# Building a scan's operands on ScalarE instead of GpSimd, in a fused Mamba2, MLP and LoRA kernel

## The chip, the cores and the metric

The kernel runs on one core of one Trainium2 chip. The metric is the device time in microseconds (us) of one execution. Three executions of the kernel before took 840.97, 840.18 and 839.14 us, median 840.18. One more execution was profiled: 837.98 us, of which 836.1 us are the span from the first to the last recorded instruction; all rows of the trace come from it.

## The reference

The input is 8 sequences of 256 tokens with 512 features. A Mamba2 block, a gated MLP and a linear layer with one of four LoRA experts per token follow each other, with residuals and normalizations. The change touches the Mamba2 block alone, in which (H = 4 heads, P = N = 128, chunks of Q = 128 tokens, and `Xc` the same for all heads):

```
z, xs, Bs, Cs, dt = split(x @ w_in.T);  xBC = silu(conv(xBC) + conv_b)
dt = softplus(dt + dt_bias);  a = dt * A;  cs = cumsum(a)
Ldec = where(tri, exp(cs[q] - cs[k]), 0);  Xdt = Xc * dt
Yd = (C @ B.T * Ldec) @ Xdt;   states = sum_q exp(cs[-1] - cs) * B * Xdt
Yo = C @ prev * exp(cs);       Y = Yd + Yo + D * xh
y = Y * silu(z) @ w_out.T
```

## The kernel before

There is one group per sequence (`GROUPS` = 8), that is two tiles of 128 tokens. Each matrix product is made of three f16 products of high and low halves. The work is a software pipeline of three stages over groups: stage a is the Mamba2 block, b the gated MLP, c the linear layer with LoRA. `first()` runs stage a of group 0 alone, together with the preparation of the weights; it is called the head below. Then `steps` runs t = 1 to 9, with a of group t, b of group t-1 and c of group t-2. Stage a exists in the head and in steps 1 to 7. Step 1 also prepares most of the MLP's weights: `prepare(f)` has ScalarE write the upper f16 halves (L560) and VectorE the lower ones (L871).

A step has FBLK = 14 blocks, f = 0 to 13. In each block TensorE makes the gate and up products of block f (`b_gu`, 24 matmuls into the PSUM banks `gu`) and then the down product of block f-1 (`b_down`, 6 matmuls into `acc`). Between them lie ScalarE's silu (L670, tile `sg`), VectorE's product (L1044), ScalarE's upper half of the activation (L680, tile `act`) and VectorE's lower half (L1049). `b_down(f)` waits for that lower half of block f (`act_ready`). The pieces of stages a and c are hung behind these in each block by the tables `A_AT` and `C_AT`, one table for each engine. All engines run their own list strictly in the order in which it is written, and semaphores tie the lists together; nothing is scheduled by a planner.

The pieces of stage a that matter here are these.

- `a_dt` on ScalarE and VectorE (f = 2) turns the projected dt into dt (`dts`) and a = dt*A (`a_t`, L978), 8 numbers in each partition: 2 tiles of 4 heads.
- `a_scan_in` on GpSimd (L453) multiplies the triangular mask `tri` by `a_t`, to `ra`, one 128x512 operation for each tile: the operand of the matmul that makes the sums of a (`a_dec` on TensorE, f = 4 and 5, which waits for `ra_ready`, and outside the head for `sz_ready`, ScalarE's silu of z, for the bank).
- `a_tdt` on GpSimd (L461) multiplies `tri` by dt, to `tdt`, which lies in the tile `hn`; VectorE multiplies it with the exponentials (`a_dec`, f = 5).
- `a_xd` on GpSimd (L469) makes D * xh, four 128x256 operations into `y`, added much later (`a_y`, f = 7, L1005).
- ScalarE has at f = 3 `a_silu(g, 2)`, `a_z(g, 1)` and `a_tok` (L608, L614, L627), and at f = 4 the two exponentials (`a_exp`, L638), for which it loads another table of functions and then the first again (ACT_TABLE_LOAD).
- `a_xw` and `a_ce` on GpSimd (L476, L484) make the operands of the state. TensorE's `a_state` (f = 6, `wa<-hn,tok`) waits for `xw_ready`.

Of the kernel before, what the change touches and what calls it, by code (L numbers as in the profile page):

```python
# [24 lines left out]
ALU = mybir.AluOpType  # L25
ACT = mybir.ActivationFunctionType
# [8 lines left out]
H = 4  # L35
# [67 lines left out]
def build(nc, x, w_in, w_dt, w_out, w_gate, w_up, w_down, w_lin, w_gl, lora_b, cols, rows, ln_rows, out):  # L103
# [3 lines left out]
    with ctx:  # L107
# [8 lines left out]
        def sem(name):  # L116
            if name not in made:
                made[name] = ctx.enter_context(nc.semaphore(name))
            return made[name]
# [199 lines left out]
        def prev(g, per, k, eng, s):  # L319

            if g > 0:
                eng.wait_ge(s, g * per - per + k)
# [94 lines left out]
        def _(pool):  # L417
# [27 lines left out]
                inv_std(chain_n, s_a[:, 1], mv_a[:, :, 1], 1.0 + EPS, EPS * EPS, sem("rstd2_a_ready"))  # L445
                inv_std(chain_n, s_a[:, 0], mv_a[:, :, 1], 1.0, EPS, sem("rstd_a_ready"))

            def a_scan_in(g):
                pool.wait_ge(sem("a_ready"), g + 1)
                for j in range(TILES):  # L450
                    if j == 0:
                        prev(g, 3, 3, pool, sem("dec_ps_ready"))
                    nc.gpsimd.tensor_tensor(ra[:, j], tri[:].unsqueeze(1).broadcast_to([P, H, P]),  # L453
                                            a_t[:, j].unsqueeze(2).broadcast_to([P, H, P]), ALU.mult)\
                        .then_inc(sem("ra_ready"), 1)

            def a_tdt(g):


                for j in range(TILES):  # L460
                    nc.gpsimd.tensor_tensor(tdt[:, j], tri[:].unsqueeze(1).broadcast_to([P, H, P]),  # L461
                                            dts[:, 4, j].unsqueeze(2).broadcast_to([P, H, P]), ALU.mult)\
                        .then_inc(sem("tdt_ready"), 1)

            def a_xd(g):
                prev(g, 2, 2, pool, sem("o_ps_ready"))
                pool.wait_ge(sem("xbc_ready"), g * 3 + 1)
                for h in range(H):
                    nc.gpsimd.tensor_scalar(y[:, h], xbc[:, 0], rowt[:, 4 + h:5 + h], None, ALU.mult)\  # L469
                        .then_inc(sem("xd_ready"), 1)  # L470

            def a_xw(g):
                pool.wait_ge(sem("w0_ready"), g + 1)
                pool.wait_ge(sem("tok_ready"), g + 1)
# [30 lines left out]
            def step(a, b, c):  # L505
                if c is not None:
                    chain_c.group(c)
                    norm_c(c, 1, 1.0)
                if b is not None:
                    b_copy(b)  # L510
                if a is not None:
                    a_xd(a)
                    a_scan_in(a)
                    a_tdt(a)
                if c is not None:
                    norm_c(c, 2, ACT_SCALE)
                if a is not None:
                    a_xw(a)
                    a_ce(a)
                    if a + 1 < GROUPS:  # L520
                        a_norm(a + 1)
                    a_rms(a)
                if c is not None:
                    norm_c(c, 3, 1.0)
                    chain_c.close()

            def first():
                a_norm(0)
                a_scan_in(0)
                a_tdt(0)  # L530
                a_xd(0)
                a_xw(0)
                a_ce(0)
                a_norm(1)
                a_rms(0)
# [6 lines left out]
        def _(eng):  # L542
# [74 lines left out]
            def a_dt(g):  # L617
# [3 lines left out]
                chain_a(nc.scalar.activation(dts[:, 2], dts[:, 1], ACT.Exp, scale=-1.0))  # L621
                nc.scalar.activation(dts[:, 3], dts[:, 2], ACT.Ln, bias=1.0).then_inc(sem("log_ready"), 1)

            def a_tok(g):
                eng.wait_ge(sem("tok_ps_ready"), g + 1)
                prev(g, 2, 2, eng, sem("y_ps_ready"))
                nc.scalar.activation(tok[:].rearrange("p m s -> p (m s)"), bank(g, 2)[:, 0:3 * P], ACT.Copy)\  # L627
                    .then_inc(sem("tok_ready"), 1)
# [72 lines left out]
            def c_u(g, j):  # L701
# [2 lines left out]

            A_AT = {0: lambda g: a_conv(g, 1), 1: lambda g: (a_conv(g, 2), a_silu(g, 0)),
                    2: lambda g: (a_silu(g, 1), a_z(g, 0), a_dt(g)),
                    3: lambda g: (a_silu(g, 2), a_z(g, 1), a_tok(g)),
                    4: lambda g: (a_exp(g, 0), a_exp(g, 1)), 6: lambda g: (a_exp(g, 2), a_state(g)),
                    8: lambda g: a_sumsq(g, 0), 9: lambda g: a_sumsq(g, 1), 11: lambda g: a_hi2(g)}
            NEXT_AT = {10: lambda g: a_hi1(g), 13: lambda g: a_conv(g, 0)}  # L710
# [21 lines left out]
            def first():  # L732
                chain_a.group(0)
                prep_a()
                a_t1(0)
                small_hi(T_IN)
                upper_halves(range(0, 9))
                a_conv(0, 0)
                upper_halves([9])
                a_dt(0)  # L740
                a_silu(0, 0)
                a_conv(0, 1)
                a_conv(0, 2)
                a_tok(0)
                a_exp(0, 0)
                a_exp(0, 1)
                a_exp(0, 2)
                a_silu(0, 1)
                a_silu(0, 2)
                a_z(0, 0)  # L750
                a_z(0, 1)
                upper_halves(range(S_GU, S_GU + 4))
                a_state(0)
                upper_halves(range(S_GU + 4, S_GU + 7))
                a_sumsq(0, 0)
                a_sumsq(0, 1)
                upper_halves(range(S_GU + 7, S_MIX))
                a_hi1(1)
                a_t2(0)
                a_conv(1, 0)  # L760
                chain_a.close()
# [857 lines left out]
```

## Time and profile before

| What | us |
|---|---|
| median of three executions | 840.18 |
| profiled execution | 837.98 |
| its span | 836.1 |
| TensorE busy | 770.9 |
| VectorE busy | 478.1 |
| ScalarE busy | 331.5 |
| GpSimd busy | 150.0 |

In the trace TensorE is PE (its weight loads PEld), VectorE DVE, ScalarE ACT and GpSimd POOL; L with a number is a line of the kernel. Step 1 runs from about 76 to 172 us. The token transposes of steps 2 to 7 start at 201.05, 296.19, 391.32, 486.46, 579.93 and 675.07 us, 95.1 us apart, and once 93.5 us. A share of busy time says little here, because each engine's list is in fixed order: what counts is, in each block, which wait ends last.

### The profile page before, as it was taken

Reading aid. Unit: us, or ns where it says so; the run is one execution under the profiler, and the core shown is the slowest. Engines: PE = TensorE matmul, PEld = TensorE weight load, DVE = VectorE, ACT = ScalarE, POOL = GpSimd, SP = SyncE. Lnnn points to the kernel's source line nnn. Section 1 sums busy time; section 2 is a strip of 40 time slices with the busy share of each in tenths; the row PEclk is TensorE's granted clock in tenths of the full one; section 3 lists DMA queues with packets and bytes.
Section 4 is the critical chain, followed back from the end, with each engine's and each line's share of the span. In section 5 each row is a group of like instructions: output and inputs, shape, how many; then the busy total and the mean of one; then the engine's idle time right before and its main releaser. Section 6 shows DMA issues by size and latency. Waiting matters only on the chain.

```text
span 836.1 us, 13857 instructions
## 1 busy us (share of the span) xinstructions
PE 770.9 (92%) x5558; PEld 540.1 (65%) x5558; DVE 478.1 (57%) x1109; ACT 331.5 (40%) x603; POOL 150.0 (18%) x197
## 2 busy tenths in 40 slices
PE   4994989999999999999999999999999999999945
PEld 3853856676657866586666866677666866577632
DVE  6874667875635665475645565465644564265163
ACT  2642676625423443324523453325523353222211
POOL 1420121214110331014110331014110320010010
PEclk9995999999999999999999999999999999999987
DMA  9931000300104020210104020210103110021010
GB/s 331 387 131 26 1 26 1 67 11 26 26 2 97 5 51 1 52 52 26 26 1 78 25 51 1 51 51 21 33 1 63 39 27 1 11 66 27 1 50 26
DMA packets 59936, 41.11 MB, mean 49 GB/s; under 512 B 45664, under 2 KB 45792, under 8 KB 59872
## 3 DMA queue, kind: packets, MB, share of 16 engines
q1 hardware_dynamic: 59872, 40.22, 17.4%
q8 instruction: 44, 0.72, 0.4%
q14 instruction: 20, 0.16, 0.1%
HBM read 25.01 MB, written 4.19 MB: 35 GB/s over the span
## 4 chain that ended last, share of the span: by engine, by line
PE 80%; DVE 10%; ACT 4%; issue 2%; DMA 2%; SPq 1%; POOL 0%; POOLq 0%; DVEq 0%; ACTq 0%
PE gu L1252 32%; PE wa L1252 22%; PE acc L1252 17%; PE wc L1252 7%; DVE xbc L944 2%; DVE weights L871 2%; ACT L621 1%; DMA weights<-in_w_in 1%; ACT silu_z L614 1%; DVE sg L1044 0%; DVE stats_c L886 0%; DVE dts L970 0%; PE wa L1340 0%; DVE h L1074 0%; DMA xa<-in_x 0%
## 5 line engine op out<-in xcount | busy, mean ns | idle before, releaser
L1252 PE MATMUL gu<-h2t,weights 128*128 128x256 f16 x2688 | 320.2, 277 | 0.0
L1252 PEld LDWEIGHTS gu<-h2t,weights 128*128 128x128 f16 x2688 | 264.5, 99 | 58.4 <-issue 19.7
L1252 PE MATMUL acc<-weights,act 128*128 128x512 f16 x672 | 163.4, 379 | 5.8 <-DVE act L1049 5.8
L1044 DVE SCALAR_TENSOR_TENSOR sg<-gu,bound,sg 128x256 f32<-128x256 f32 x112 | 53.7, 480 | 136.9 <-ACT sg L670 136.8
L670 ACT ACTIVATE sg<-gu,scale_inv 128x256 f32<-128x256 f32 x112 | 52.9, 472 | 172.9 <-PE gu L1252 172.8
L1252 PE MATMUL wa<-ht,weights 128*128 128x256 f16 x912 | 110.3, 280 | 5.3 <-DMA ht<-ra 5.3
L1252 PEld LDWEIGHTS wa<-ht,weights 128*128 128x128 f16 x912 | 91.4, 100 | 23.9 <-DMA ht<-ra 5.7
L1252 PEld LDWEIGHTS acc<-weights,act 128*128 128x128 f16 x672 | 65.3, 98 | 63.2 <-DVE act L1049 7.9
L680 ACT ACTIVATE act<-sg 128x256 f16<-128x256 f32 x112 | 46.6, 416 | 98.4 <-DVE sg L1044 97.6
L1049 DVE TENSOR_TENSOR act<-sg,act 128x256 f16<-128x256 f32 x112 | 52.0, 464 | 54.0 <-ACT act L680 54.0
L944 DVE SCALAR_TENSOR_TENSOR xbc<-wa,conv_ws,xbc 128x253 f32<-128x253 f32 (+1 forms) x132 | 57.3, 475 | 3.0 <-ACT xbc L597 1.5
L439 POOL TENSOR_SCALAR small_c<-mv_c 128x2 f32<-128x2 f32 x24 | 4.6, 191 | 303.3 <-DVE mv_c L888 303.3
L1252 PE MATMUL wa<-w_out_t,y 128*128 128x512 f32 x128 | 57.4, 592 | 0.0
L871 DVE SCALAR_TENSOR_TENSOR weights<-weights,scale_v 128x512 f16<-128x512 f32 x56 | 41.1, 790 | 15.6 <-ACT weights L560 15.5
L469 POOL TENSOR_SCALAR y<-xbc,rows_t 128x256 f32<-128x256 f32 x32 | 36.1, 1140 | 43.9 <-ACT xbc L608 43.9
L597 ACT ACTIVATE xbc<-wa,cols_t,conv_ws 128x256 f32<-128x256 f32 x48 | 24.4, 559 | 47.2 <-PE wa L1252 47.2
L1252 PEld LDWEIGHTS wa<-w_out_t,y 128*128 128x128 f32 x128 | 24.2, 190 | 25.5 <-issue 23.4
L1252 PE MATMUL wc<-weights,h3t 128*128 128x512 f16 x168 | 38.5, 379 | 0.0
L560 ACT ACTIVATE weights<-weights,scale_v 128x512 f16<-128x512 f32 x56 | 36.2, 711 | 0.9 <-DVE scale_v L821 0.5
L648 ACT ACTIVATE hn<-h 128x512 f32<-128x512 f32 x16 | 10.1, 631 | 61.5 <-DVE h L1012 61.5
L1012 DVE TENSOR_TENSOR h<-wa,h 128x512 f32<-128x512 f32 x16 | 11.0, 690 | 35.3 <-PE wa L1252 35.3
L453 POOL TENSOR_TENSOR ra<-tri,a_t 128x512 f32<-128x512 f32 x16 | 17.2, 1094 | 68.9 <-DVE a_t L978 68.9
(194 smaller groups left out, 790.4 us busy)
## 6 DMA issues: line engine op xcount, KB each, us to landing
xa<-in_x SPq DMA_DIRECT2D x8, 512.0 KB, 3.5
weights<-in_x SPq DMA_DIRECT2D x8, 512.0 KB, 3.7
out_x<-h SPq DMA_DIRECT2D x16, 256.0 KB, 2.2
weights<-in_w_in SPq DMA_DIRECT2D x5, 512.0 KB, 6.5
weights<-in_w_down SPq DMA_DIRECT2D x3, 768.0 KB, 13.2
weights<-in_w_gate SPq DMA_DIRECT2D x2, 1024.0 KB, 12.7
weights<-in_w_up SPq DMA_DIRECT2D x2, 1024.0 KB, 14.1
weights<-in_w_gate SPq DMA_DIRECT2D x2, 768.0 KB, 14.3
```

What stands on the lines that cost most here:

```text
L453: nc.gpsimd.tensor_tensor(ra[:, j], tri[:].unsqueeze(1).broadcast_to([P, H, P]), a_t[:, j].unsqueeze(2).broadcast_to([P, H, P]), ALU.mult)\
L469: nc.gpsimd.tensor_scalar(y[:, h], xbc[:, 0], rowt[:, 4 + h:5 + h], None, ALU.mult)\
L560: nc.scalar.activation(Wh[:, u, 0], W[:, u + SHIFT], ACT.Copy, scale=sv[:, t:t + 1])\
L597: nc.scalar.activation(xbc[:, c], src[:, m * SEQ:(m + 1) * SEQ], ACT.Identity, bias=conv_b[:, c:c + 1], scale=cw[:, c * TAPS + TAPS - 1:c ...
L670: nc.scalar.activation(sg[:, f % 2], GU[f % 2][:, 0:SEQ], ACT.Silu, scale=inv_gate)\
L680: nc.scalar.activation(act[:, slot(f), 0], sg[:, f % 2], ACT.Copy)\
L871: nc.vector.scalar_tensor_tensor(Wh[:, u, 1], W[:, u + SHIFT], sv[:, t:t + 1], Wh[:, u, 0], ALU.mult, ALU.subtract).then_inc(split, 1)
L944: ins = nc.vector.scalar_tensor_tensor(xbc[:, c, late:], conv_in(g, c)[:, 0:SEQ - late], cw[:, c * TAPS + k:c * TAPS + k + 1], xbc[:, c, l ...
L1012: nc.vector.tensor_tensor(h01[:, j], o_bank(g, j)[:], h01[:, j], ALU.add)\
L1044: nc.vector.scalar_tensor_tensor(sg[:, f % 2], GU[f % 2][:, SEQ:2 * SEQ], up_to_act, sg[:, f % 2], ALU.mult, ALU.mult).then_inc(sem("prod_ ...
L1049: nc.vector.tensor_tensor(act[:, slot(f), 1], sg[:, f % 2], act[:, slot(f), 0], ALU.subtract)\
L1252: return nc.tensor.matmul(dst, left, right, start=start, stop=stop)
```

## The change

`a_scan_in`, `a_tdt` and `a_xd` leave GpSimd's list and enter ScalarE's. ScalarE takes a scale for each partition, so each head and tile becomes an operation of its own: 8 copies of 128x128 for `ra`, 8 for `tdt`, and 4 of 128x256 for D * xh. GpSimd keeps `a_xw`, `a_ce`, the copies of `h1b` and the small powers. In the steps all 20 copies stand at f = 3: 16 ahead of `a_silu(g, 2)` and 4 behind `a_tok`. In the head the 16 stand between `a_tok` and the first exponential, the 4 behind `a_z`. The wait of `a_scan_in` for `dec_ps_ready` of the group before is gone. The lists of TensorE, VectorE and SyncE are unchanged.

```diff
--- before.py
+++ after.py
@@ -445,30 +445,6 @@
                 inv_std(chain_n, s_a[:, 1], mv_a[:, :, 1], 1.0 + EPS, EPS * EPS, sem("rstd2_a_ready"))
                 inv_std(chain_n, s_a[:, 0], mv_a[:, :, 1], 1.0, EPS, sem("rstd_a_ready"))
 
-            def a_scan_in(g):
-                pool.wait_ge(sem("a_ready"), g + 1)
-                for j in range(TILES):
-                    if j == 0:
-                        prev(g, 3, 3, pool, sem("dec_ps_ready"))
-                    nc.gpsimd.tensor_tensor(ra[:, j], tri[:].unsqueeze(1).broadcast_to([P, H, P]),
-                                            a_t[:, j].unsqueeze(2).broadcast_to([P, H, P]), ALU.mult)\
-                        .then_inc(sem("ra_ready"), 1)
-
-            def a_tdt(g):
-
-
-                for j in range(TILES):
-                    nc.gpsimd.tensor_tensor(tdt[:, j], tri[:].unsqueeze(1).broadcast_to([P, H, P]),
-                                            dts[:, 4, j].unsqueeze(2).broadcast_to([P, H, P]), ALU.mult)\
-                        .then_inc(sem("tdt_ready"), 1)
-
-            def a_xd(g):
-                prev(g, 2, 2, pool, sem("o_ps_ready"))
-                pool.wait_ge(sem("xbc_ready"), g * 3 + 1)
-                for h in range(H):
-                    nc.gpsimd.tensor_scalar(y[:, h], xbc[:, 0], rowt[:, 4 + h:5 + h], None, ALU.mult)\
-                        .then_inc(sem("xd_ready"), 1)
-
             def a_xw(g):
                 pool.wait_ge(sem("w0_ready"), g + 1)
                 pool.wait_ge(sem("tok_ready"), g + 1)
@@ -508,10 +484,6 @@
                     norm_c(c, 1, 1.0)
                 if b is not None:
                     b_copy(b)
-                if a is not None:
-                    a_xd(a)
-                    a_scan_in(a)
-                    a_tdt(a)
                 if c is not None:
                     norm_c(c, 2, ACT_SCALE)
                 if a is not None:
@@ -526,9 +498,6 @@
 
             def first():
                 a_norm(0)
-                a_scan_in(0)
-                a_tdt(0)
-                a_xd(0)
                 a_xw(0)
                 a_ce(0)
                 a_norm(1)
@@ -621,6 +590,27 @@
                 chain_a(nc.scalar.activation(dts[:, 2], dts[:, 1], ACT.Exp, scale=-1.0))
                 nc.scalar.activation(dts[:, 3], dts[:, 2], ACT.Ln, bias=1.0).then_inc(sem("log_ready"), 1)
 
+            def a_scan_in(g):
+                eng.wait_ge(sem("a_ready"), g + 1)
+                for j in range(TILES):
+                    for h in range(H):
+                        ins = nc.scalar.activation(ra[:, j, h], tri[:], ACT.Copy, scale=a_t[:, j, h:h + 1])
+                    ins.then_inc(sem("ra_ready"), 1)
+
+            def a_tdt(g):
+
+                for j in range(TILES):
+                    for h in range(H):
+                        ins = nc.scalar.activation(tdt[:, j, h], tri[:], ACT.Copy, scale=dts[:, 4, j, h:h + 1])
+                    ins.then_inc(sem("tdt_ready"), 1)
+
+            def a_xd(g):
+                prev(g, 2, 2, eng, sem("o_ps_ready"))
+                eng.wait_ge(sem("xbc_ready"), g * 3 + 1)
+                for h in range(H):
+                    nc.scalar.activation(y[:, h], xbc[:, 0], ACT.Copy, scale=rowt[:, 4 + h:5 + h])\
+                        .then_inc(sem("xd_ready"), 1)
+
             def a_tok(g):
                 eng.wait_ge(sem("tok_ps_ready"), g + 1)
                 prev(g, 2, 2, eng, sem("y_ps_ready"))
@@ -704,7 +694,7 @@
 
             A_AT = {0: lambda g: a_conv(g, 1), 1: lambda g: (a_conv(g, 2), a_silu(g, 0)),
                     2: lambda g: (a_silu(g, 1), a_z(g, 0), a_dt(g)),
-                    3: lambda g: (a_silu(g, 2), a_z(g, 1), a_tok(g)),
+                    3: lambda g: (a_scan_in(g), a_tdt(g), a_silu(g, 2), a_z(g, 1), a_tok(g), a_xd(g)),
                     4: lambda g: (a_exp(g, 0), a_exp(g, 1)), 6: lambda g: (a_exp(g, 2), a_state(g)),
                     8: lambda g: a_sumsq(g, 0), 9: lambda g: a_sumsq(g, 1), 11: lambda g: a_hi2(g)}
             NEXT_AT = {10: lambda g: a_hi1(g), 13: lambda g: a_conv(g, 0)}
@@ -742,6 +732,8 @@
                 a_conv(0, 1)
                 a_conv(0, 2)
                 a_tok(0)
+                a_scan_in(0)
+                a_tdt(0)
                 a_exp(0, 0)
                 a_exp(0, 1)
                 a_exp(0, 2)
@@ -749,6 +741,7 @@
                 a_silu(0, 2)
                 a_z(0, 0)
                 a_z(0, 1)
+                a_xd(0)
                 upper_halves(range(S_GU, S_GU + 4))
                 a_state(0)
                 upper_halves(range(S_GU + 4, S_GU + 7))
```

The changed kernel's rows carry its own line numbers (its L660 is L670 before, for example). First ScalarE at blocks f = 3 and 4 of step 2 (`sg` is the MLP's silu, `act` its activation's upper half, `xbc` the convolution's silu, `dec` the exponentials). Before:

```order
L670 ACTIVATE sg<-gu,scale_inv 128x256
L680 ACTIVATE act<-sg 128x256
L608 ACTIVATE xbc<-xbc 128x512
L614 ACTIVATE silu_z<-wa,scale_inv 128x512
L627 ACTIVATE tok<-wa 128x384
L670 ACTIVATE sg<-gu,scale_inv 128x256
L680 ACTIVATE act<-sg 128x256
L638 ACT_TABLE_LOAD
L638 ACTIVATE dec<-wa 128x512 x2
```

And in the changed kernel:

```order
L660 ACTIVATE sg<-gu,scale_inv 128x256
L670 ACTIVATE act<-sg 128x256
L597 ACTIVATE ra<-tri,a_t 128x128 x8
L604 ACTIVATE hn<-tri,dts 128x128 x8
L577 ACTIVATE xbc<-xbc 128x512
L583 ACTIVATE silu_z<-wa,scale_inv 128x512
L617 ACTIVATE tok<-wa 128x384
L611 ACTIVATE y<-xbc,rows_t 128x256 x4
L660 ACTIVATE sg<-gu,scale_inv 128x256
L670 ACTIVATE act<-sg 128x256
L628 ACT_TABLE_LOAD
L628 ACTIVATE dec<-wa 128x512 x2
```

Twenty operations more stand between the `act` of block 3 and the `sg` of block 4. In steps 3 to 7 the piece reads the same, and in step 1 three `weights` operations stand behind `tok` before and behind `y` now.

Then ScalarE in the head, from the copy of the transposed tokens (`tok`) to that of the state (`act<-wa`, L643 before). Before:

```order
L627 ACTIVATE tok<-wa 128x384
L638 ACT_TABLE_LOAD
L638 ACTIVATE dec<-wa 128x512 x2
L638 ACTIVATE act<-wa 128x512
L608 ACT_TABLE_LOAD
L608 ACTIVATE xbc<-xbc 128x512 x2
L614 ACTIVATE silu_z<-gu,scale_inv 128x512 x2
L560 ACTIVATE weights<-weights,scale_v 128x512 x4
L643 ACTIVATE act<-wa 128x512
```

And in the changed kernel:

```order
L617 ACTIVATE tok<-wa 128x384
L597 ACTIVATE ra<-tri,a_t 128x128 x8
L604 ACTIVATE hn<-tri,dts 128x128 x8
L628 ACT_TABLE_LOAD
L628 ACTIVATE dec<-wa 128x512 x2
L628 ACTIVATE act<-wa 128x512
L577 ACT_TABLE_LOAD
L577 ACTIVATE xbc<-xbc 128x512 x2
L583 ACTIVATE silu_z<-gu,scale_inv 128x512 x2
L611 ACTIVATE y<-xbc,rows_t 128x256 x4
L529 ACTIVATE weights<-weights,scale_v 128x512 x4
L633 ACTIVATE act<-wa 128x512
```

The table load for the exponentials, which stood right behind `tok`, now stands behind the sixteen copies, and the four copies for `y` stand ahead of the weights' halves.

## Rows read from the trace of the kernel before

**Rows 1.** The page: busiest engine, and the chain that ended last, by engine.
```profile
PE 770.9 (92%) x5558; PEld 540.1 (65%) x5558; DVE 478.1 (57%) x1109; ACT 331.5 (40%) x603; POOL 150.0 (18%) x197
...
PE 80%; DVE 10%; ACT 4%; issue 2%; DMA 2%; SPq 1%; POOL 0%; POOLq 0%; DVEq 0%; ACTq 0%
```
**Rows 2.** Waits of PE: for whom, us in total, times, longest.
```profile
PE wa L1340 <- DVE xbc L944: 14.5, 7, 2.1
```
**Rows 3.** PE timeline, step 3: start, us, instructions, [idle before <-releaser].
```profile
296.54 4.45 PE L1252 MATMUL gu<-h2t,weights 128*128 128x256 f16 x24
...
306.46 1.46 PE L1252 MATMUL acc<-weights,act 128*128 128x512 f16 x6
...
312.09 1.46 PE L1252 MATMUL acc<-weights,act 128*128 128x512 f16 x6
...
314.25 1.02 PE L1252 MATMUL wa<-hn,tok 128*128 128x512 f32 x2
```
**Rows 4.** ACT timeline, step 3: the silu of blocks 4 and 5.
```profile
301.03 0.47 ACT L670 ACTIVATE sg<-gu,scale_inv 128x256 f32<-128x256 f32 x1 [2.68 <-PE gu L1252]
...
307.21 0.47 ACT L670 ACTIVATE sg<-gu,scale_inv 128x256 f32<-128x256 f32 x1
```
**Rows 5.** DVE and POOL timelines, step 3, block 5.
```profile
308.69 0.43 DVE L1049 TENSOR_TENSOR act<-sg,act 128x256 f16<-128x256 f32 x1 [0.48 <-ACT act L680]
...
310.00 1.54 POOL L476 TENSOR_TENSOR hn<-tok,w 128x512 f32<-128x512 f32 x1 [8.68 <-DVE w L992]
```
**Rows 6.** ACT groups by form: xcount, busy us, mean ns of one, idle before.
```profile
L680 ACT ACTIVATE act<-sg 128x256 f16<-128x256 f32 x112 | 46.6, 416 | 98.4 <-DVE sg L1044 97.6 <-PE acc L1252 0.8
...
L581 ACT ACTIVATE ra<-dec,small_a 128x512 f16<-128x512 f32 x14 | 9.2, 710 | 0.0
...
L686 ACT ACTIVATE weights<-h 128x512 f16<-128x512 f32 x14 | 8.0, 629 | 0.9 <-DVE h L1074 0.9
...
L552 ACT ACTIVATE gl_w<-h3t 128x144 f16<-128x144 f32 x1 | 0.3, 322 | 1.3 <-DVE h3t L848 1.3
```
**Rows 7.** ACT timeline, head: two scaled copies in a row.
```profile
67.67 1.32 ACT L581 ACTIVATE ra<-dec,small_a 128x512 f16<-128x512 f32 x2
```
**Rows 8.** Windows of steps 3 and 5 (third from last: PEclk), ACT and PE timelines of step 5.
```profile
296.00:302.00 6.00, 5.81 (x33) 4.16 (x34) 4.18 (x10) 2.36 (x5) 2.47 (x4) 0.72 0.29 90
...
486.00:492.00 6.00, 5.54 (x36) 3.96 (x37) 5.00 (x12) 3.43 (x7) 2.75 (x4) 1.00 0.23 81
...
489.64 0.47 ACT L670 ACTIVATE sg<-gu,scale_inv 128x256 f32<-128x256 f32 x1 [1.01 <-PE gu L1252]
...
502.86 1.02 PE L1252 MATMUL wa<-hn,tok 128*128 128x512 f32 x2
```
**Rows 9.** Timelines of step 1: DVE, POOL, ACT and PE, blocks 3 to 6.
```profile
109.24 3.27 DVE L871 SCALAR_TENSOR_TENSOR weights<-weights,scale_v 128x512 f16<-128x512 f32 x3
...
115.46 2.08 DVE L871 SCALAR_TENSOR_TENSOR weights<-weights,scale_v 128x512 f16<-128x512 f32 x3 [0.75 <-ACT weights L560]
...
108.81 2.49 POOL L461 TENSOR_TENSOR hn<-tri,dts 128x512 f32<-128x512 f32 x2
...
126.70 1.55 POOL L476 TENSOR_TENSOR hn<-tok,w 128x512 f32<-128x512 f32 x1 [15.41 <-DVE w L992]
...
116.55 0.46 ACT L670 ACTIVATE sg<-gu,scale_inv 128x256 f32<-128x256 f32 x1
...
125.88 1.47 PE L1252 MATMUL acc<-weights,act 128*128 128x512 f16 x6 [0.58 <-DVE act L1049]
...
128.39 1.10 PE L1252 MATMUL wa<-hn,tok 128*128 128x512 f32 x2 [0.19 <-POOL hn L476]
```
**Rows 10.** ACT and PE timelines, head: table load, first exponential, attention products.
```profile
36.25 1.28 ACT L638 ACT_TABLE_LOAD   x1
39.86 0.60 ACT L638 ACTIVATE dec<-wa 128x512 f32<-128x512 f32 x1 [2.33 <-PE wa L1252]
...
44.88 1.96 PE L1252 MATMUL wa<-xbc 128*128 128x512 f32 x4 [0.19 <-ACT xbc L608]
```

## The prediction

> **What bounds the kernel now.** I read the page first. TensorE is busy for 92% of the span, and 80% of the chain that ended last is TensorE's own work [rows 1]. So its list is almost never empty, and time is lost where it waits. The view of waits gives the one wait of the steady steps: seven times about 2.1 us at the token transposes, for VectorE's convolution [rows 2], which follows the dt chain of block 2. GpSimd has no part in it. So the work that the change takes from GpSimd is not what TensorE waits for, and the question is what the same work does to ScalarE.
>
> For this I read the timelines of one steady step (step 3, blocks 3 to 6). ScalarE sits idle 2.68 us before the silu of block 4 [rows 4]. Its silu of block 5 starts at 307.21, the lower half of that block's activation is done at 308.69 + 0.43 = 309.12 on VectorE [rows 5], and TensorE asks for it at 312.09 [rows 3]: a margin of 2.9 us, not counting 0.07 us of signal. Behind this, GpSimd's first product for the state runs from 310.00 to 311.54 [rows 5] and TensorE's state matmul stands at 314.25 [rows 3]. These margins are what the change spends.
>
> **The price of the new operations.** The trace has no 128x128 copy on ScalarE with a scale for each partition. The rows around it give one [rows 6]: a plain copy takes 629 ns at 512 columns and 416 at 256, so 0.83 ns for a column and 203 ns fixed; at 128 columns that is 309 ns (the 128x144 copy, 322 ns, lies on this line). The same 512 columns with a scale from a tile take 710, that is 81 ns more. So one copy lasts about 390 ns at 128 columns and 497 at 256. Two scaled copies in a row take 1.32 us and not 1.42 [rows 7]: back to back each costs 0.10 us less. I take 0.29 us for a 128x128 copy and 0.40 for a 128x256 one. From below: the scale might cost nothing on these shapes, then 0.21 and 0.32. From above: the plain 128x144 copy plus 0.10 for the scale, less only 0.09 of overlap, 0.33, and 0.42 for the larger. My values lie on the line through four rows, so I stay with them. The insertion at block 3 is X = 16 x 0.29 + 4 x 0.40 = 6.24 us (4.6 to 7.0 by the bounds).
>
> **The head.** Here the table load for the exponentials ran at 36.25, while ScalarE would have waited anyway, and 2.33 us of idling were left before the first exponential [rows 10]. Now 16 x 0.29 = 4.64 us come first and the load behind them. The exponential moves by 4.64 - 2.33 = 2.31 us. The third exponential, the second table load and the silu follow in a row, and TensorE's attention products waited for that silu even before, by 0.19 us at 44.88 [rows 10]. TensorE's list is in order, so everything behind moves: **+2.31**. The four copies for D stand in front of weights' halves and a state copy that waits for TensorE anyway: nothing. VectorE's convolution, relieved of GpSimd beside it, ends earlier, but then waits for TensorE's gram products: nothing.
>
> **Step 1.** ScalarE has no idle time here: the weights' halves fill it, and the silu of block 4 starts at 116.55 with no gap [rows 9]. TensorE already waits 0.58 us for the activation of block 5 at 125.88, and 0.19 us for GpSimd's product at 128.39 [rows 9]. So all of X reaches TensorE. One thing comes back. GpSimd's multiplication of the mask by dt ran at 108.81 beside three of VectorE's lower halves, which took 3.27 us where the same three take 2.08 at 115.46 [rows 9]. They stood ahead of the product of block 3, and ScalarE waited for it before its next work. That is -1.19 us. Step 1: 6.24 - 1.19 = **+5.05**.
>
> **Steps 2 to 7.** In step 3 TensorE runs the gate and up product of block 4 in 4.45 us [rows 3]. The granted clock in that window is 0.72 of full speed, in step 5 it is 1.00 [rows 8], after the same wait of 2.1 us: the clock fell to 1.2 GHz in the one and stayed at 2.4 GHz in the other. Windows at steps 2, 4, 6 and 7 read much like step 3. So there are five steps of one kind and one of the other.
>
> With the drop: the silu of block 4 had 2.68 us of idling before it, 2.78 with the overlap that copies in a row regain. It moves by 6.24 - 2.78 = 3.46 us. The activation of block 4 has about 3.5 us to TensorE's 306.46 [rows 3] and is just in time. Everything to block 5's silu is one row of ScalarE work with two table loads, so that silu goes to 307.21 + 3.46 = 310.67. The down product of block 5 finds its operand at 309.12 + 0.07 + 3.46 = 312.65 and not at 312.09: +0.6. The state matmul needs GpSimd's product, which ended at 311.54 and took 0.14 us to be seen (126.70 + 1.55 to 128.39 in step 1 [rows 9]). It now comes at 311.68 + 3.46 = 315.14, against 314.25: **+0.89** in all for the step. Nothing gives it back: up to the next transposes TensorE was never idle, and the dt chain that these wait for starts from TensorE's own products.
>
> Without the drop (step 5): the idle time before the silu of block 4 was only 1.01 us [rows 8], 1.11 with the overlap. The silu moves by 5.13, from 489.64 to 494.77; block 5's silu follows 6.18 us later as in step 3 (307.21 - 301.03 [rows 4]), at 500.95; the state's operand follows 311.68 - 307.21 = 4.47 us behind that, at 505.42, against 502.86 [rows 8]: **+2.56**. A step with the drop was 1.7 us longer than one without, and the added costs differ by as much: both kinds become equally long, because ScalarE's row of work sets the end in each.
>
> **Sum.** 2.31 + 5.05 + 5 x 0.89 + 2.56 = 14.4 us. On the profiled execution that is 837.98 + 14.4 = 852.4, on the median of the runs, 2.2 us higher, 854.6. With the low prices (X = 4.6): head 16 x 0.21 - 2.33 = 1.0, step 1 3.4, steps with the drop 0 (they cost from X = 5.35 on), step 5 0.9, together 5.4. With the high prices (X = 7.0): 2.95 + 5.8 + 5 x 1.65 + 3.3 = 20.3. These ends are 845.6 and 860.5.
>
> **Rivals.**
> *The new copies are cheaper* and the margins of steps 2 to 7 hold. For it: no row shows a small scaled copy, and the margin is missed by less than 1 us. Against it: four rows lie on one line. Price: +5.4, so 845.6; it holds while X is under 5.35.
>
> *The clock pays too.* In step 1 TensorE would wait for the second sum (its bank is freed by the silu of z, now behind the 16 copies), for block 4 and for block 5, some 3.2, 2.5 and 2.3 us within 17. After one wait of 2.1 us it fell to half rate in five of seven cases, and 24 matmuls then took 4.45 us for 2.78 (the row at 296.54 [rows 3]). A drop under ScalarE's row costs nothing, since TensorE then waits less; one behind it costs 1.67 us. At four to seven more of these: +7 to +12, so 862 to 867. Against it: the new waits of the steady steps are below 1 us. The Trainium skill, TensorE: Matmul & The Clock Gate, section HAM oscillation, says that idle gaps inside a loop make the engine fall back to half rate every time round. By this rule it could be paid in each step; no row shows it after a wait as short as the new ones.
>
> *Faster: VectorE gains what GpSimd gives up, and ScalarE's insertion hides.* One place on the path pays, the three halves of step 1: -1.19, so 839.0. It decides only if X in step 1 is below 1.19 us, that is 0.06 us a copy, and the head's sixteen fit into 2.33 us. Against it stands every row of ScalarE. The Trainium skill speaks for this rival: GPSIMD Engine Reference, section Specifications, says that GpSimd shares its SBUF interfaces with VectorE and contends with instructions that have two SBUF inputs or run in a two-port mode. The 3.27 against 2.08 us agree with it. But in steps 2 to 7 it meets only work with slack, or with an operand in PSUM.
>
> *Nothing to see*: waits that I take for binding are not, and slack elsewhere swallows all: within 1.7 us of 840.18. Only GpSimd's own path could hide that much, and it is not in the chain [rows 1].
>
> **Chances.** Forecast (850 to 860.5, its own mechanism at prices near mine) 0.70; cheaper copies (843 to 850) 0.14; clock (above 860.5) 0.11; no difference 0.03; faster 0.02. A change of 0.2%, 1.7 us, is about what a measurement of this kernel can tell. So faster 0.02, same 0.03, slower 0.95. The range takes in the bounds of the copies' prices, 846 to 861.
>
> **What would show it.** ScalarE's groups should have 128 copies of 128x128 at about 390 ns and 32 of 128x256 at about 500. PE should get a new wait for ACT at the first attention products in the head, of 2.5 us; in step 1 waits for VectorE's `act` before the down products of blocks 4 and 5; in each later step about 0.6 us before the down product of block 5 and 0.3 before the state matmul. Steps 2 to 7 should all be 96.0 us long, with a clock drop or without. The three lower halves at block 3 of step 1 should take 2.08 us. The forecast is wrong if the steady steps keep 95.1 us (the copies are cheap), or if they reach 98 (clock, or a link of the row that I hold to be free).

## The result and the profile after

The changed kernel takes 854.64 us in the median of four executions (854.21 to 855.14). The kernel before took 839.66 in the four executions beside it. The ratio is 1.0186, 95% interval 1.0152 to 1.0219: slower by 1.5 to 2.2%. The profiled execution took 854.21 us, span 852.5, against 837.98 and 836.1 before.

The chain's shares by engine, and TensorE's waits, on the page and in the view of waits:

```profile
PE 773.1 (91%) x5558; PEld 537.1 (63%) x5558; DVE 471.5 (55%) x1109; ACT 381.1 (45%) x763; POOL 79.8 (9%) x133
...
PE 66%; ACT 14%; DVE 12%; issue 4%; DMA 2%; POOL 2%; SPq 1%; POOLq 0%; DVEq 0%; ACTq 0%
```
```profile
PE wa L1333 <- DVE xbc L937: 14.6, 7, 2.1
...
PE acc L1245 <- DVE act L1042: 8.0, 12, 1.6
PE wa L1245 <- ACT silu_z L583: 7.8, 5, 3.0
...
PE wa L1245 <- ACT dec L628: 2.2, 1, 2.2
...
PE wa L1245 <- POOL hn L452: 1.3, 7, 0.2
```

GpSimd lost 70 us of work and ScalarE won 50. TensorE's share of the chain fell from 80% [rows 1] to 66%, and ScalarE's rose from 4 to 14%. The wait of [rows 2] is unchanged. What is new are waits for ScalarE, directly (`silu_z`, `dec`) or through VectorE and GpSimd, which only pass its delay on. The five waits for `silu_z` are one of 2.97 us in step 1 and one of 1.2 us in each of the four later steps whose clock did not drop.

ScalarE's new groups by form (xcount | busy us, mean ns):

```profile
L597 ACT ACTIVATE ra<-tri,a_t 128x128 f32<-128x128 f32 x64 | 19.4, 386 | 0.0
L604 ACT ACTIVATE hn<-tri,dts 128x128 f32<-128x128 f32 x64 | 19.4, 386 | 0.0
...
L611 ACT ACTIVATE y<-xbc,rows_t 128x256 f32<-128x256 f32 x32 | 13.6, 498 | 0.0
```

Back to back, eight of the small ones take 2.43 us, 0.292 each beyond the first, and four of the large ones 1.70, 0.40 each. So X, the prediction's name for the length of all 20 copies in the row of block 3, was 6.27 us.

Step 3 on TensorE, and the silu of blocks 4 and 5 on ScalarE, as in [rows 3] and [rows 4]:

```profile
306.06 4.45 PE L1245 MATMUL gu<-h2t,weights 128*128 128x256 f16 x24
...
322.17 1.47 PE L1245 MATMUL acc<-weights,act 128*128 128x512 f16 x6 [0.39 <-DVE act L1042]
...
324.69 0.67 PE L1245 MATMUL wa<-hn,tok 128*128 128x512 f32 x1 [0.19 <-POOL hn L452]
```
```profile
314.04 0.46 ACT L660 ACTIVATE sg<-gu,scale_inv 128x256 f32<-128x256 f32 x1
...
320.21 0.47 ACT L660 ACTIVATE sg<-gu,scale_inv 128x256 f32<-128x256 f32 x1
```

ScalarE's silu of block 4 has no idle time in front of it any more. The two new waits of TensorE are those that the margins of [rows 5] let expect. The printed idle is shorter than the real delay, because a row's printed length reaches past the start of the next row (24 matmuls are printed as 2.78 us and the next row starts 2.62 behind them). From start to start the two delays are 0.55 and 0.36 us, and with the state matmuls, which are 0.08 us longer, 0.99 in all.

The table takes the time from the token transposes of one step to those of the next as the length of a step. A clock drop, here and below, is a stretch in which the clock granted to TensorE fell to its lower level (1.2 GHz) behind the transposes.

| Stretch | before | after | difference | predicted |
|---|---|---|---|---|
| start to the head's transposes | 35.21 | 35.62 | +0.4 | 0 |
| from there to step 1's (rest of the head, start of step 1) | 74.26 | 77.29 | +3.0 | +2.3 |
| step 1 to 2 | 91.58 | 96.67 | +5.1 | +5.05 |
| step 2 to 7, five | 474.02 | 480.67 | +6.65 | +6.1 |
| step 7 to the end | 161.03 | 162.25 | +1.2 | +0.9 |

The sum is 16.4 us in these two profiled executions, and 15.0 between the medians. All five steps after are 96.12 to 96.14 us long, although behind the transposes the clock fell in steps 3 and 4 and in none of the other five (windows at steps 3 and 5, granted clock third from last; compare [rows 8]):

```profile
306.00:312.00 6.00, 6.00 (x34) 4.14 (x32) 2.78 (x7) 6.00 (x19) 0.88 (x2) 0.72 0.26 90
...
498.00:505.00 7.00, 5.78 (x36) 3.84 (x37) 3.00 (x8) 6.75 (x21) 0.88 (x2) 1.00 0.29 76
```

Step 1 on VectorE and TensorE, to be read with [rows 9]:

```profile
112.68 2.07 DVE L864 SCALAR_TENSOR_TENSOR weights<-weights,scale_v 128x512 f16<-128x512 f32 x3
```
```profile
116.11 1.47 PE L1245 MATMUL acc<-weights,act 128*128 128x512 f16 x6
...
121.41 1.15 PE L1245 MATMUL wa<-ra,below 128*128 128x512 f32 x2 [2.97 <-ACT silu_z L583]
122.37 4.45 PE L1245 MATMUL gu<-h2t,weights 128*128 128x256 f16 x24
127.40 1.47 PE L1245 MATMUL acc<-weights,act 128*128 128x512 f16 x6 [0.58 <-DVE act L1042]
...
134.38 1.47 PE L1245 MATMUL acc<-weights,act 128*128 128x512 f16 x6 [1.17 <-DVE act L1042]
```

The lower halves are back at 2.07 us with GpSimd silent. With that a wait of TensorE ahead of the down product of block 3 is gone, which the kernel before had:

```profile
113.86 1.47 PE L1252 MATMUL acc<-weights,act 128*128 128x512 f16 x6 [1.25 <-DVE act L1049]
```

The wait for the bank (2.97 us) was followed by a fall of the clock (granted clock 0.72 from 121 to 127 us). The 24 matmuls behind it took 4.45 us and not 2.78, and that filled most of what would have been the next wait.

The head, on ScalarE and TensorE, to be read with [rows 10]:

```profile
38.88 2.43 ACT L604 ACTIVATE hn<-tri,dts 128x128 f32<-128x128 f32 x8
41.33 1.28 ACT L628 ACT_TABLE_LOAD   x1
42.62 1.09 ACT L628 ACTIVATE dec<-wa 128x512 f32<-128x512 f32 x2
```
```profile
43.27 1.52 PE L1245 MATMUL wa<-ra,ones 128*128 128x512 f32 x2 [2.18 <-ACT dec L628]
...
45.44 3.69 PE L1245 MATMUL gu<-ht,weights 128*128 128x256 f16 x24
```

The table load, once inside ScalarE's idle time, now stands behind the copies, and TensorE waits 2.18 us for the first exponential. Behind that wait the clock fell too (granted clock 0.82 from 40 to 46 us): the 24 matmuls took 3.69 us for 2.78, and the rows in front of them were slower as well. From the head's transposes to the attention products it is 13.34 us (35.62 to 48.96), and was 9.67 before (35.21 to 44.88): 3.7 us more, of which some 1.3 are the clock. The trace of the run with D*xh back on GpSimd, described below, has the same wait without the fall:

```profile
44.36 1.12 PE L1247 MATMUL wa<-ra,ones 128*128 128x512 f32 x2 [2.18 <-ACT dec L631]
...
45.76 2.78 PE L1247 MATMUL gu<-ht,weights 128*128 128x256 f16 x24
48.73 1.96 PE L1247 MATMUL wa<-xbc 128*128 128x512 f32 x4 [0.19 <-ACT xbc L587]
```

There it is 12.02 us (36.71 to 48.73), 2.35 more than before.

### The profile page after: what moved, and what is told of

It is laid out like the page before. It is cut to its first block, busy times and chain, and to the rows that moved or that the text cites. A ratio compares the mean times of both kernels' runs of the same rounds, so it can differ in the third digit from the quotient of the medians.

```text
span 852.5 us, 13946 instructions
## 1 busy us (share of the span) xinstructions
PE 773.1 (91%) x5558; PEld 537.1 (63%) x5558; DVE 471.5 (55%) x1109; ACT 381.1 (45%) x763; POOL 79.8 (9%) x133
## 4 chain that ended last, share of the span: by engine, by line
PE 66%; ACT 14%; DVE 12%; issue 4%; DMA 2%; POOL 2%; SPq 1%; POOLq 0%; DVEq 0%; ACTq 0%
PE gu L1245 26%; PE wa L1245 19%; PE acc L1245 14%; PE wc L1245 7%; DVE xbc L937 2%; ACT hn L604 2%; ACT ra L597 2%; DVE sg L1037 1%; DVE weights L864 1%; ACT y L611 1%; POOL hn L452 1%; ACT L628 1%; ACT L660 1%; ACT L590 1%; ACT silu_z L583 1%
## 5 line engine op out<-in xcount | busy, mean ns | idle before, releaser
L1245 PE MATMUL gu<-h2t,weights 128*128 128x256 f16 x2688 | 316.8, 275 | 0.0
L660 ACT ACTIVATE sg<-gu,scale_inv 128x256 f32<-128x256 f32 x112 | 52.9, 472 | 132.2 <-PE gu L1245 131.2
L670 ACT ACTIVATE act<-sg 128x256 f16<-128x256 f32 x112 | 46.6, 416 | 112.3 <-DVE sg L1037 112.3
L1042 DVE TENSOR_TENSOR act<-sg,act 128x256 f16<-128x256 f32 x112 | 47.7, 426 | 54.1 <-ACT act L670 54.1
L864 DVE SCALAR_TENSOR_TENSOR weights<-weights,scale_v 128x512 f16<-128x512 f32 x56 | 38.7, 747 | 21.9 <-ACT weights L529 21.8
L1245 PEld LDWEIGHTS wc<-weights,h3t 128*128 128x128 f16 x168 | 16.4, 98 | 19.8
```

The lines of the kernel that those rows point to most:

```text
L660: nc.scalar.activation(sg[:, f % 2], GU[f % 2][:, 0:SEQ], ACT.Silu, scale=inv_gate)\
L670: nc.scalar.activation(act[:, slot(f), 0], sg[:, f % 2], ACT.Copy)\
L864: nc.vector.scalar_tensor_tensor(Wh[:, u, 1], W[:, u + SHIFT], sv[:, t:t + 1], Wh[:, u, 0], ALU.mult, ALU.subtract).then_inc(split, 1)
L1042: nc.vector.tensor_tensor(act[:, slot(f), 1], sg[:, f % 2], act[:, slot(f), 0], ALU.subtract)\
L1245: return nc.tensor.matmul(dst, left, right, start=start, stop=stop)
```

## Experiments

Two theories were tested. "Row" is the prediction's: ScalarE's work of block 3 is one uninterrupted row, and its length X, against fixed margins, sets the cost. "Share" is that each copy on ScalarE costs its part wherever it stands. Times are medians; ratio is against runs of the kernel before on the same chip (838.3 to 839.2 us, 839.66 for the changed kernel). What is said of single steps comes from one profiled execution of each kernel.

| Kernel | us | ratio (95%) | step with / without clock drop |
|---|---|---|---|
| before | 839.66 | 1 | 95.1 / 93.5 |
| changed | 854.64 | 1.0186 (1.0152 to 1.0219) | 96.1 / 96.1 |
| D*xh back on GpSimd | 845.98 | 1.0089 (1.0065 to 1.0112) | 95.1 / 94.95 |
| only D*xh on ScalarE | 838.66 | 0.9993 (0.9983 to 1.0003) | 95.1 / 93.5 |
| D*xh at block 5 | 846.94 | 1.0092 (1.0072 to 1.0112) | 95.1 / 94.96 |
| and the 16 copies last | 843.70 | 1.0076 (1.0048 to 1.0103) | 95.1 / 94.5 |
| eight copies more | 873.18 | 1.0409 (1.0393 to 1.0426) | 99.0 in all |
| head as before | 852.21 | 1.0161 (1.0136 to 1.0186) | 96.1 / 96.1 |
| tdt held in step 1 | 837.00 | 0.9981 (0.9966 to 0.9997) | 95.1 / 93.5 |
| before, turned | 815.29 | 0.9719 (0.9696 to 0.9743) | no drop, 91.2 |
| changed, turned | 835.22 | 0.9964 (0.9947 to 0.9980) | no drop, 93.5 |
| before, turned and held | 815.69 | 0.9734 (0.9710 to 0.9759) | no drop, 91.2 |

**D*xh back on GpSimd.** `a_xd` as before, `a_scan_in` and `a_tdt` on ScalarE.

> The changed kernel, with D*xh given back to GpSimd (32 copies of 128x256 less on ScalarE; the 128 copies of 128x128 stay). Theory 'row': ScalarE's insertion at block 3 has the length X, 6.27 us in the changed kernel and 16 x 0.292 = 4.67 us here. A step with a clock drop pays only what is above 5.35, so nothing: steps of 95.1 us; one without a drop pays X - 3.68 = 1.0. The head still pays its 3.0 us, step 1 pays 4.67 - 1.19 = 3.5. Sum 6.5 to 9 us over the kernel before, about 847. Theory 'share' (each copy on ScalarE costs its share wherever it stands, 14 to 16 us over 160 copies, 0.1 us each): 128 copies, 12 us over before, about 852.

7.5 us over before (5.5 to 9.4), as "row" says and not the 12 of "share". One fifth of the copies, a quarter of X, carried half of the cost, because it was the part above the margin. The one step without a drop took 94.95 us, where 94.5 were expected (see D*xh at block 5).

**Only D*xh on ScalarE.**

```diff
-                    a_xd(a)
...
-                a_xd(0)
...
-                    3: lambda g: (a_silu(g, 2), a_z(g, 1), a_tok(g)),
+                    3: lambda g: (a_silu(g, 2), a_z(g, 1), a_tok(g), a_xd(g)),
...
+                a_xd(0)
```

> The kernel before, with D*xh alone moved to ScalarE (32 copies of 128x256, behind a_tok at block 3, behind a_z in the head). Theory 'row': X = 1.6 us. Step 1, where ScalarE has no idle time, pays 1.6; the head and steps 2 to 7 pay nothing (95.1 us, or 93.5 where the clock does not fall). About +1.6 us over before. Theory 'share': 32 copies at 0.1 us, +3.2 us, spread over head and steps: steps of 95.5 us.

The trace has what was expected: step 1 is 203.83 - 110.66 = 93.17 us and was 91.58, the others are unchanged.

```profile
110.66 0.52 PE L1339 MATMUL wa<-ident,xbc 128*128 128x128 f32 x3 [2.08 <-DVE xbc L943]
...
203.83 0.52 PE L1339 MATMUL wa<-ident,xbc 128*128 128x128 f32 x3 [2.08 <-DVE xbc L943]
```

The time has not: 0.6 us less than before (1.4 less to 0.3 more), where 1.6 more was expected. In the profiled execution two of steps 2 to 7 had no clock drop and not one, which is 1.7 us. Whether the later steps go without it more often in this kernel is not settled, since only profiled executions show single steps.

**D*xh at block 5.** The same 160 copies.

```diff
-                    3: lambda g: (a_scan_in(g), a_tdt(g), a_silu(g, 2), a_z(g, 1), a_tok(g), a_xd(g)),
-                    4: lambda g: (a_exp(g, 0), a_exp(g, 1)), 6: lambda g: (a_exp(g, 2), a_state(g)),
+                    3: lambda g: (a_scan_in(g), a_tdt(g), a_silu(g, 2), a_z(g, 1), a_tok(g)),
+                    4: lambda g: (a_exp(g, 0), a_exp(g, 1)), 5: lambda g: a_xd(g),
+                    6: lambda g: (a_exp(g, 2), a_state(g)),
```

> The changed kernel with the same 160 copies, but in the steps the four for D*xh stand at block 5, behind the activation of block 5, where ScalarE was idle for 3.6 us. Theory 'row': the row up to the state's operand loses 1.6 us, so X = 4.67 in front of it: steps with a drop 95.1 us, without 94.5, step 1 pays 3.5 and the head 3.0 as in the kernel with D*xh on GpSimd: about 847, 6.5 to 9 us over before. Theory 'share': no change against the changed kernel, 854.6, steps of 96.1.

7.7 us less than the changed kernel with as many copies: "share" is out. One number was off. Steps without a drop took 94.96 us, not 94.5, and the timeline of TensorE in step 6 names another link, the wait for the silu of z that frees the bank:

```profile
588.75 0.52 PE L1334 MATMUL wa<-ident,xbc 128*128 128x128 f32 x3 [2.09 <-DVE xbc L938]
...
595.25 1.13 PE L1246 MATMUL wa<-ra,below 128*128 128x512 f32 x2 [1.22 <-ACT silu_z L583]
...
683.71 0.52 PE L1334 MATMUL wa<-ident,xbc 128*128 128x128 f32 x3 [2.09 <-DVE xbc L938]
```

**The 16 copies last**, behind `a_silu`, `a_z` and `a_tok`, with D*xh at block 5. Against the changed kernel:

```diff
-                    3: lambda g: (a_scan_in(g), a_tdt(g), a_silu(g, 2), a_z(g, 1), a_tok(g), a_xd(g)),
-                    4: lambda g: (a_exp(g, 0), a_exp(g, 1)), 6: lambda g: (a_exp(g, 2), a_state(g)),
+                    3: lambda g: (a_silu(g, 2), a_z(g, 1), a_tok(g), a_scan_in(g), a_tdt(g)),
+                    4: lambda g: (a_exp(g, 0), a_exp(g, 1)), 5: lambda g: a_xd(g),
+                    6: lambda g: (a_exp(g, 2), a_state(g)),
```

> The changed kernel with D*xh at block 5, and at block 3 the 16 copies behind a_silu(g, 2), a_z(g, 1) and a_tok instead of ahead of them. The amount of work up to the silu of block 4 is the same as with D*xh at block 5 alone (X = 4.67), only the silu of z, which frees the bank of TensorE's second sum, comes 4.7 us earlier. Two links are to be told apart for a step without a clock drop, which took 94.96 us there. If the bank is the link (wait of 1.22 us), it becomes 93.5 + (4.67 - 3.68) = 94.5 us and the wait is gone; steps with a drop stay at 95.1. If the row to the state's operand is the only link, nothing changes. In all about 846, 0 to 2 us less than with D*xh at block 5 alone.

Step 6 is now 681.97 - 587.44 = 94.53 us, and the bank's wait is gone; the block-5 wait is what is left:

```profile
587.44 0.52 PE L1334 MATMUL wa<-ident,xbc 128*128 128x128 f32 x3 [2.08 <-DVE xbc L938]
...
602.29 1.47 PE L1246 MATMUL acc<-weights,act 128*128 128x512 f16 x6 [0.38 <-DVE act L1043]
...
681.97 0.52 PE L1334 MATMUL wa<-ident,xbc 128*128 128x128 f32 x3 [2.08 <-DVE xbc L938]
```

So there are two links: the silu of z behind the 16 copies, which sets a step without a drop at X = 4.67, and the row to the state's operand, which sets the changed kernel's steps. In all the kernel is 3.2 us quicker than with D*xh at block 5 alone, where 0 to 2 were expected. Three steps without a drop explain 0.4 us each, 1.3 together. In the profiled executions 0.8 us more lie ahead of step 1's transposes, where the clock fell in the head of that run (24 matmuls in 4.43 us) and not of this one (2.78), and 1.2 behind step 7's, for a cause that is open.

**Eight copies more**, into a spare tile that nobody reads.

```diff
...
+                    for j in range(TILES):
+                        for h in range(H):
+                            nc.scalar.activation(spare[:, j, h], tri[:], ACT.Copy, scale=a_t[:, j, h:h + 1])\
...
```

> The changed kernel with eight more 128x128 copies a step (into a spare f16 tile, read by nobody) behind the eight for ra, steps 1 to 7 only. Theory 'row': above the knee each us of X is a us of step: 8 x 0.292 = 2.34 us for each of seven steps, 16.4 over the changed kernel, 871; steps 2 to 7 of 98.5 us each, with a clock drop or without. Theory 'share': 56 copies at 0.1 us, +5.6, 860.

18.5 us over the changed kernel, 16.4 expected. A step takes 98.97 us, 2.84 more for 2.34 us of copies. The rest is the first link and the clock, as steps 2 and 4 show:

```profile
222.58 1.71 PE L1253 MATMUL wa<-ra,below 128*128 128x512 f32 x2 [3.55 <-ACT silu_z L584]
224.09 3.92 PE L1253 MATMUL gu<-h2t,weights 128*128 128x256 f16 x24
...
411.68 0.52 PE L1341 MATMUL wa<-ident,xbc 128*128 128x128 f32 x3 [2.08 <-DVE xbc L945]
...
510.65 0.52 PE L1341 MATMUL wa<-ident,xbc 128*128 128x128 f32 x3 [2.08 <-DVE xbc L945]
```

Behind the transposes TensorE waits once, 3.55 us for the silu of z, and in each of steps 2 to 7 the clock falls behind that wait (granted clock 0.72 from 222 to 228 us; the 24 matmuls take 3.92 to 3.99 us and not 2.78). No wait at block 5 is left to absorb this. The sum fits the first link: 94.96 us, the length that it set at 16 copies, plus 2.34 for eight more and 1.67 for a drop is 98.97. So the prediction's clock rival came true here. The changed kernel's waits of 1.2 us for the same silu did not set it off.

**Head as before.**

> The changed kernel with the head as before: in group 0 GpSimd makes the sixteen operands and D*xh, ScalarE only from group 1 on. Theory 'row': the head's part is 4.67 - 2.33 = 2.3 us, and the changed kernel's trace shows another 0.7 to 0.9 us there, 24 matmuls at the lower clock (3.69 us for 2.78) behind the new wait. So 3 us less than the changed kernel, 851.6, with nothing changed behind the head. Rival 'absorbed': if the head's shift were taken up by its transfers and preparations, nothing would be gained, 854.6.

2.4 us less than the changed kernel, where 3 were expected, and between the transposes of head and step 1 the traces show 74.56 us against 77.29. So the head's part reaches the end, and "absorbed" is out. Its size is not the same in every execution: the same stretch took 75.55 and 75.74 us in the two profiled executions whose clock did not fall in the head (D*xh back on GpSimd, the 16 copies last) and 78.22 and 78.31 in two where it fell further (D*xh at block 5, eight copies more), against 74.26 before.

**Tdt held in step 1.** The kernel before, with one wait. "Neighbour" is the theory that VectorE's lower halves were slow because GpSimd worked beside them.

```diff
             def a_tdt(g):
+                if g == 1:
+                    pool.wait_ge(sem("prod_ready"), 4)
```

> The kernel before with one wait more: in step 1 GpSimd makes tdt only after VectorE's product of block 3. Theory 'neighbour': the three lower halves of L871 (L872 or so) take 2.1 and not 3.3 us because GpSimd no longer works beside them; the activation of block 3 is ready 1.2 us earlier and, since ScalarE has no slack in step 1, the time falls by 1.2 us, 838.0. Rival: they are slow for another reason (the weights' own transfers), then 3.3 us stays and 839.2.

VectorE's, GpSimd's and TensorE's timelines, step 1:

```profile
111.06 2.07 DVE L871 SCALAR_TENSOR_TENSOR weights<-weights,scale_v 128x512 f16<-128x512 f32 x3
...
114.84 1.71 DVE L920 TENSOR_SCALAR h<-xa,mv_a,small_a 128x512 f32<-128x512 f32 x2
```
```profile
113.60 2.21 POOL L461 TENSOR_TENSOR hn<-tri,dts 128x512 f32<-128x512 f32 x2 [2.93 <-DVE sg L1044]
```
```profile
111.29 0.85 PE L1340 MATMUL wa<-ident,xbc 128*128 128x128 f32 x3 [2.08 <-DVE xbc L944]
111.93 4.16 PE L1252 MATMUL gu<-h2t,weights 128*128 128x256 f16 x24
...
202.05 0.52 PE L1340 MATMUL wa<-ident,xbc 128*128 128x128 f32 x3 [2.07 <-DVE xbc L944]
```

The three lower halves fall to 2.07 us, and now L920 beside GpSimd is slow (1.71 us, 1.00 alone). GpSimd's nearness was the cause of their length. The time is 1.6 us less (0.3 to 2.9), but that is no clean measure of what it costs: in the profiled execution step 1 is 0.8 us shorter (90.76 for 91.58), with a clock drop at its start that the kernel before did not have there, and one more of the later steps had no drop.

**The turn.** VectorE's convolution ahead of its dt chain, in both kernels.

```diff
...
-                    2: lambda g: (a_dt(g), a_conv(g, 2)), 3: lambda g: a_h0(g),
+                    2: lambda g: (a_conv(g, 2), a_dt(g)), 3: lambda g: a_h0(g),
...
```

> The kernel before, with VectorE's order at block 2 turned round: the convolution's last third first, then the dt chain, which waits for ScalarE. The convolution then runs in VectorE's idle 5.6 us, and the token transposes of TensorE find it done. Expected: the wait of 2.08 us goes in all seven steps, and with it the drop of the clock behind it (1.67 us in five of six steps): steps 2 to 7 of 91.4 us, step 1 shorter by 2.5, in all 839.2 - 23.4 = 815.8. Rival: the dt chain ends later and a new wait (ScalarE's activation of block 3, or ra) takes the place of the old one: 5 to 10 us gained.

> The changed kernel with the same turn of VectorE's order. Theory 'row': TensorE's new margin is ScalarE's row from the activation of block 3 to the state's operand, and this row starts only 2.5 us earlier than before the turn, while TensorE would be 3.75 us earlier. So a step does not become 91.4 but 93.7 us long; the cost of the change grows from 1.0 to 2.3 us a step, in all 837, that is some 21 us above the kernel before with the same turn. Rival: were the cost of the change a fixed amount, 15 us, this run would show 831.

Transposes of steps 3 and 4 of the turned kernel before, and of the turned changed kernel:

```profile
289.79 0.49 PE L1340 MATMUL wa<-ident,xbc 128*128 128x128 f32 x3
381.00 0.49 PE L1340 MATMUL wa<-ident,xbc 128*128 128x128 f32 x3
```
```profile
299.50 0.49 PE L1333 MATMUL wa<-ident,xbc 128*128 128x128 f32 x3
...
393.04 0.49 PE L1333 MATMUL wa<-ident,xbc 128*128 128x128 f32 x3
```

The wait of [rows 2] is gone in both kernels, and with it every clock drop of steps 2 to 7 (the granted clock of the turned kernel before is 1.00 from 195 to 745 us): steps of 91.2 us, 815.29 in all, 23.6 under the kernel before. With the change, steps take 93.5 us (93.7 expected). The change costs 19.9 us in this company (21 expected) and cost 15.0 before. A margin was used up, not an amount of work paid.

**Turned and held.** The turned kernel before; in step 1 GpSimd makes `ra` and `tdt` only when the activation of block 3 is complete (`act_ready` 4).

> The kernel before with the turn of VectorE's order, and in step 1 GpSimd makes ra and tdt only when the activation of block 3 is ready. In the turned kernel the three lower halves beside GpSimd took 3.63 us and the activation's lower half 1.30 us, for 2.08 and 0.43 alone, ahead of a wait of 2.17 us of TensorE for that activation. Theory 'neighbour': both fall to their own times, 2.4 us less in step 1, so 815.3 - 2.4 = 812.9. Rival: TensorE then waits for ra instead, and half or less of it is gained.

815.69 us, no difference from the turned kernel, where 2.4 less were expected. VectorE and TensorE in step 1:

```profile
106.66 2.07 DVE L873 SCALAR_TENSOR_TENSOR weights<-weights,scale_v 128x512 f16<-128x512 f32 x3
...
111.69 4.31 DVE L873 SCALAR_TENSOR_TENSOR weights<-weights,scale_v 128x512 f16<-128x512 f32 x3
```
```profile
117.36 1.47 PE L1254 MATMUL acc<-weights,act 128*128 128x512 f16 x6 [0.94 <-DVE act L1051]
...
124.34 1.47 PE L1254 MATMUL acc<-weights,act 128*128 128x512 f16 x6 [1.17 <-DVE act L1051]
```

The first three are quick (3.63 us in the turned kernel), but GpSimd's five microseconds now lie beside the next three, which take 4.31, and TensorE, which waited 2.17 us for block 3 in the turned kernel, waits 0.94 us for block 4 and 1.17 for block 5. The collision moved. Nor does TensorE wait for `ra`, as the rival had it: its row that needs `ra` has no idle time in front.

## Why the prediction was right

The forecast was 854.6, the measured median 854.64. Against the runs beside it the change costs 15.0 us, where 14.4 were forecast. The mechanism was the forecast one: ScalarE's row from the copies of block 3 to the state's operand sets the end of a step, whatever the clock does, and moving a part of the copies out of that row took the cost away by the forecast amount.

- **Prices.** 0.29 and 0.40 us back to back were measured as 0.292 and 0.40; the line through four rows held. X was 6.27 and not 6.24.
- **Head.** +3.0 against +2.31. The mechanism (the table load leaves the idle time) held: where the clock did not fall, the attention products came 2.35 us later. The term missed the clock, some 1.3 us behind the new wait in the changed kernel's trace. Up to step 1's transposes 0.6 to 1.1 us come back, most of it in 24 matmuls at the start of step 1 (4.91 us for 5.30); the prediction did not see this either, and no run shows its cause. The prediction looked for the wait at the attention products; it is at the third sum, for the first exponential.
- **Step 1.** +5.09 against +5.05, with the lower halves 1.2 us quicker as forecast (2.07 for 3.27) and the wait at block 3 gone. Holding `tdt` alone showed their cause, not by itself the size of what comes back. Of the three waits the first was near the forecast (2.97 for 3.2). The later ones were 0.6 and 1.2 and not 2.5 and 2.3. The clock fell ahead of the second, under ScalarE's row, and took 1.67 us of it. The clock does not explain the third. The three forecast waits add up to 8.0 us, more than the +5.05 and the waits already there (1.25 and 0.58), 6.9 together; measured are 4.7 us of waits and 1.67 of clock. The list of waits was too high, the term was not.
- **Steady steps.** +0.99 with a drop, against +0.89, +2.67 without, against +2.56, and both kinds of step became equal, at 96.1 us. That the state's operand is the link of the changed kernel was right. That it is the only one was not: at X = 4.67 us and without a drop the silu of z decides, 94.96 us for the 94.5 of the row alone. Of the prediction's low end, at X = 4.6, the 0.9 us for step 5 were therefore too little.
- **Clock rival.** In the profiled executions the drops behind the transposes did not grow in number (two of six steps, five before), and they cost the steady steps nothing. A small part of the rival came true in the head, as said, and with eight copies more all of it in each step.
- **Faster rival.** Its mechanism is real: 1.2 us on VectorE in step 1. Nothing of it is seen in the steady steps: their sum came out without it.

The agreement to 0.04 us is luck: the median of before moved between 838.3 and 840.2 from one set of runs to another, and the two profiled executions differ by 16.2 us, so that the forecast for the profiled one (852.4) was 1.8 below the measured 854.21, with the terms of the head and of steps 2 to 7 all somewhat low.

## What to carry to other kernels

Before moving work to an idler engine, find where in its list it will stand, sum it with what stands beside it without a gap, and compare with the margin of the next consumer: 20% of the copies, moved two blocks on, took away half of the loss. A table load that hid in idle time comes to light when work is put ahead of it. Look first at the wait that the profile does name: turning two calls on VectorE was worth 23.6 us, and it also took away the slack under which the change had looked cheap.

## What the runs showed of the hardware

- After a wait of 2.08 us TensorE's clock fell to its lower level (1.2 GHz) in five of six steps before and two of six after, and the next 24 matmuls took 4.45 us for 2.78; after waits of 3.55 us it fell in all six. After waits of 1.2 us, in the changed kernel, it did not. A drop costs 1.67 us where TensorE is the bound (95.14 us for 93.47), and nothing where it would wait anyway (96.1 us with and without); without the wait of 2.08 us, in the turned kernels, none of steps 2 to 7 had one.
- Three of VectorE's scaled differences of two SBUF operands take 2.07 us alone and 3.27, 3.63 and 4.31 beside GpSimd's products; a tensor-scalar pair goes from 1.00 to 1.71. Six of the convolution's operations, with one operand in PSUM, took 2.67 us beside GpSimd (before, step 1, at 106.65 us) and as much with GpSimd silent (after, step 1, at 110.09 us).
